# One hybrid transformer block on one core: the interleaving tables of all five engines written anew

## The reference

```
x = x + deltanet(layernorm(x))      # 8 heads of 16, two decaying states per head, scan over the tokens, own output norm
x = x + layernorm(x) @ sign(W).T
x = x + attention(layernorm(x))     # 16 heads of 8, rotary q and k, causal softmax, projection
x = x + layernorm(x) @ sign(W).T
```

## Time and profile before

| | |
|---|---|
| median of three executions | 686.31 us |
| all three | 686.31, 685.63, 686.48 us |
| span of the profiled execution, first to last instruction | 679.2 us |
| what the median has beyond that span | 7.1 us |
| TensorE busy (matmul) | 587.1 us, 86% |
| VectorE | 542.6 us, 80% |
| ScalarE | 414.9 us, 61% |
| GpSimd | 216.5 us, 32% |
| share of the last-ending chain: TensorE, VectorE, issue, DMA | 34%, 27%, 14%, 9% |
| mean granted TensorE clock | 0.955 |

### The profile page before, as it was taken

One profiled execution on the slowest core, in us unless ns is written; L12 is line 12 of the kernel. 1 busy time (PEld: TensorE's weight loads), 2 busy tenths in 40 slices (PEclk: granted clock), 3 DMA queues, 4 the chain that ended last, 5 costly groups with the idle time before them and its releaser, 6 DMA issues.

```text
span 679.2 us, 16869 instructions
## 1 busy us (share of the span) xinstructions
PE 587.1 (86%) x6352; PEld 338.2 (50%) x6352; DVE 542.6 (80%) x1547; ACT 414.9 (61%) x884; POOL 216.5 (32%) x255
## 2 busy tenths in 40 slices
PE   3686876888989899999999999999999999788995
PEld 2344534445545555555644655464646554434543
DVE  5677774889877988889899879898799877966842
ACT  2754652545777467864795767775695566346583
POOL 5261631353243251434432521535033531000000
PEclk9689787599989999999999999999999999979999
DMA  3710027000460035201540054005400433054000
GB/s 118 120 22 1 17 74 111 7 18 2 92 112 6 10 82 90 47 3 34 104 88 1 27 111 77 15 10 112 76 15 27 83 57 46 18 103 74 18 19 15
DMA packets 24914, 35.07 MB, mean 52 GB/s; under 512 B 4857, under 2 KB 22265, under 8 KB 22521
## 3 DMA queue, kind: packets, MB, share of 16 engines
q1 hardware_dynamic: 24834, 34.01, 25.4%
HBM read 22.85 MB, written 8.39 MB: 46 GB/s over the span
## 4 chain that ended last, share of the span: by engine, by line
PE 34%; DVE 27%; issue 14%; DMA 9%; POOL 7%; ACT 6%; SPq 2%; POOLq 0%; DVEq 0%; ACTq 0%
DVE mrow L1679 8%; DMA qs<-consts_bf 7%; PE ps L1215 5%; PE ps L1167 4%; PE ps L912 4%; DVE qkf L1629 3%; PE ps L1199 2%; PE ps L1196 2%; PE ps L1169 2%; PE ps L992 2%; SPq L543 2%; DVE am L1504 2%; POOL xe L624 2%; PE ps L907 2%; DMA scratch<-parts 1%
## 5 line engine op out<-in xcount | busy, mean ns | idle before, releaser
L1679 DVE TENSOR_REDUCE mrow<-ps 128x1 f32<-128x384 f32 (+3 forms) x352 | 220.5, 634 | 66.6 <-PE ps L1169 64.2
L873 ACT ACTIVATE pT<-ps 128x512 f32<-128x512 f32 (+1 forms) x330 | 173.9, 556 | 94.9 <-PE ps L1199 84.4
L1167 PE MATMUL ps<-ks,qs 72*128 72x128 bf16 (+2 forms) x384 | 101.2, 284 | 25.1 <-DVE mrow L1679 23.3
L1169 PE MATMUL ps<-ks,qs 123*128 123x128 bf16 x512 | 92.2, 226 | 6.2 <-DMA qs<-consts_bf 4.6
L1199 PE MATMUL ps<-qs,ks 75*128 75x256 bf16 (+2 forms) x384 | 93.8, 276 | 0.0
L1196 PE MATMUL ps<-qs,ks 123*128 123x128 bf16 x512 | 88.7, 223 | 5.2 <-ACT pT L873 2.4
L1215 PE MATMUL ps<-pT,va 128*32 128x512 f32 (+1 forms) x960 | 89.4, 449 | 1.8 <-DVE xk L1736 0.7
L636 POOL TENSOR_TENSOR spread<-state,cst 128x144 f32<-128x144 f32 x112 | 47.3, 444 | 121.1 <-DVE state L1533 85.1
L1167 PEld LDWEIGHTS ps<-ks,qs 72*128 72x128 bf16 x384 | 36.8, 98 | 96.7 <-DVE mrow L1679 85.8
L1196 PEld LDWEIGHTS ps<-qs,ks 123*128 123x128 bf16 x512 | 45.4, 98 | 60.9 <-ACT pT L873 26.3
L593 POOL TENSOR_TENSOR mid_rstd<-mid_ve,half 128x4 f32<-128x4 f32 x24 | 28.7, 1194 | 138.5 <-DVE mid_ve L1317 138.5
(11 more groups left out here) (209 smaller groups left out, 1091.5 us busy)
## 6 DMA issues: line engine op xcount, KB each, us to landing
ks<-scratch SPq DMA_DIRECT2D x48, 192.0 KB
scratch<-parts SPq DMA_DIRECT2D x48, 128.0 KB, 1.8
qs<-scratch SPq DMA_DIRECT2D x32, 128.0 KB
qs<-scratch SPq DMA_DIRECT2D x16, 192.0 KB
x<-x SPq DMA_DIRECT2D x8, 256.0 KB, 3.3
qs<-scratch SPq DMA_DIRECT2D x32, 64.0 KB
out<-xk SPq DMA_DIRECT2D x8, 256.0 KB, 2.3
qs<-pT SPq DMA_DIRECT2D x3, 384.0 KB, 9.2
```

Source lines behind the costliest of these rows:

```text
L873: act.activation(probs(b, g, kt)[:, c0:c0 + m, :], ps[:, score_bank(b, n), 0:m * width].rearrange("p (m n) -> p m n", n=width), ACT.Exp, s ...
L1167: pe.matmul(o[:, 0:qt * P], qs[0:K_MAX, f % RING, h, own_tile], ks[0:K_MAX, f % RING, h, 0:qt * P], start=True, stop=True, skip_group_chec ...
L1169: mm = pe.matmul(o[:, own_tile], qs[0:K_DIAG, f % RING, h, own_tile], ks[0:K_DIAG, f % RING, h, own_tile], start=True, stop=True, skip_gro ...
L1679: dve.tensor_reduce(mrow[:, qt, h0:h0 + m], ps[:, max_banks(b)[n % len(max_banks(b))], 0:m * width].rearrange("p (m k) -> p m k", k=width) ...
```

## The change

All five strings are written anew. They hold the same letters, each as often, so every step is done once, on the same engine, with the same instructions and waits; only its place among the other streams' steps is another. Nothing else differs, except that `SP_ORDER` now fills three lines of the file, so each later line has a number two higher (L1169 before is L1171 now). On each engine the coarse order stays: which batch is in which stream beside which other. On TensorE 763 of 1285 steps stand in short stretches in which the order differs, on VectorE 705 of 1073, on ScalarE 309 of 708, on GpSimd 101 of 176 and on SyncE 20 of 96. Most are swaps over one to five steps; the norm steps (n) of batches 4 to 7 move furthest.

One row of ScalarE's string, the one in which the n of batch 7 stands (the last n of the string, before and now), and the string of SyncE:

```
 ACT_ORDER = (
...
-    "ssmasassasssssaaasaaaamaaasamxssamseanssaessamamsamaassaaaaaasaaxamasaaaaaaasasaassaamasasaassaasasasasa"
+    "asssaasssssssaasaaaaaaamasamaxsssemassseaasammamsaaaassaaaaasaanxamsaaaaaaasaasaassaaamassasasaasasasasa"
...
-SP_ORDER = "nxnmmmmmmmmnxmmmmmmmxnmxmmammmmmxnmxammmmmmmxnmxmmmmmammxnmxmammmmmmxmxmmmmmammxmmxmmmmmmxmxaxaa"
+SP_ORDER = (
+    "nnxmmmmmmmmnxmmmmmmmxnmxmammmmmmxnmxmmmammmmxnmxmmmmmammxnmxmmmmmammxmxmmmmmmmaxmxmmmmmmmxmxxaaa"
+)
```

More of the change, by code:

```diff
@@ new lines @@
+    "sxsaexsaexsaaxsxxssxsxaaaxasaaxsxaxasxasxaxaaaxmasxmxaasxaaxaaaaxsxasaxamxaaaxaasaxasxaasxaxassxmxaaaxas"
+    "xaaxasaxsasxaasxasaaxssxaaxaamxaaxsexmsssxsxsexmxsxsxesxasxsasaxexsxssxsxesxesaxasxaaxaxaasaxasxmxssxaaa"
+    "saaxamsamaaxaasasaaamxasxaaaxaaamsxasxaxsaaxasaxaaxasxaxasxsxaaxmsaxmaxasaaaxasxmxaaxasasxaasxssexssxsmx"
+    "esxsxeasxeaxsssxessaxesxsxasxssxaaxaaxasaxsaxsaaxsxaaxaamxaasaxaxamaaxsaaaxasxaaaaxasxamaxaaxaxasaamxaas"
+    "xsxaxxassxaaxsxsaaxsaxaaaxsaaxaaxamsxaaxsemsxxsxemxssssexasxasexmaexsxsxaaexssxsaxasxsxasaxsaxsxasxsaxsx"
@@ new lines @@
+    "snmsmmmmmmsmsssssssssssssssssssssxsxxssxsxsxmxsxsmxmmxmxsxsxmxssxsmxsxmxssxsmmxssxssmxxxxxsnmsnxsxsssxns"
+    "snmxsxmmmxsxssxssxssmxmxmsxssxmmxmxssmxssxxxmssxmxmsssmxxsxxxmmsmmxxsxmmxnxsxxsxmsxmxsmmmxsmxxxsxssxssns"
+    "xsaxamxmasxmxaxxxxsxmmxnsxasxsssxsaxanaaxmxssxaxxsssxsxsxsxmxssxsxsxxmxmxssmxxsxmxxmmmxmxssxsxssxmnxsxsm"
+    "xmxmxxmxsxsnxmssxxmsmxsxxnsxxaxaxxnmxsxsmsxsxssxaaxmxsxsmxssxssxssxasxaxaaaxmxamxsxsxsssssxxxsssmxsxxssx"
+    "xxmmmmmsmmmssxsmxssxnxmsmxsxmxmxmnmxnxmsxxsxnsxsxmxmxmxsxmxmxssxxxxxssssaxassxaaxsxmsxaxasssxsassxsaaxxs"
@@ L133 @@
+    "axxsxssxsxmssxxssxssxxxxxxxxmmsmmssmxmxmxmxmxssxsxssmxnxsxsmxxxxmxmxsxmmsmxsxsxsnxxxnxaxaxmmxmxassxamsxm"
+    "xsassxssxaxanmaaxsxaxssxsxssxssxxsxsxxsxsssxssmxxxxsxsssxmxmxmmsxmsxsxmxmxxssxsxsxsxmxmsxsmmxxmxmxmmmxsx"
+    "sxxxxxssaxasmmxssamxamxmxmxsxasxsaxssxasxsxaasxxaxsxsxsssxsxmxssxssxssxxxssxxssssxxmxmmxmxmmxmxmxmmmxxmx"
+    "mxmmxmxxxxxmxmxmxxaxaxmxmaxaxmxmxaxaxmxaaaxmxaxmxmxxxxxxxxxxxxxxxxxxxxxxxxxxxxxxxxxxxxxxxxxxxaaxxaxaxxxx"
+    "xxxxxxxxxxxxxxxxxaaaaaaaaaaaaaaaa"
 )
 POOL_ORDER = (
-    "nnssssnssnsssssmnmsssmsssssssnnsxssmnssssmssnsmnsxsmmmmmnsnssmsmssssmasmsmnmsxmnmssmnsssssmssnammmssxmnm"
```

46 lines of the change are left out of this document (16 added, 30 removed).

## The result

The changed kernel takes 716.58 us (median of four runs, 715.06 to 723.77), the kernel before 685.97 beside it: a ratio of 1.0496, 95% interval 1.0433 to 1.0558. It is slower by some 31 us, and 27 us above the upper end of the predicted range.

A forecast was written before the change was run, and what follows sets the result against it. Only idle time could be won, at most TensorE's 92.1 us of 679.2. Terms 0.75 - 0.8 - 0.5 + 0 - 1.0 + 0 - 0.8 = -2.35 us took the median 686.31 to 684.0 us, range 679.0 to 690.0.

The forecast's parts named there:

- GpSimd costed at nothing: Scan 0: GpSimd's norm step of batch 1 moves behind two spread steps, claimed to cost nothing.
- Scan 0, masks on ScalarE: Scan 0: the mask copy now stands between the last `qM` and `qp`, delaying `am`; +0.75 us, bounds 0 and 1.00.
- Rotary tables: Scan 0, VectorE: table work of 0.92 us moves behind the next state update; -0.8 us, bounds 0 and -0.92.
- xn on ScalarE: Scan 0: xn of batch 1 (1.64 us) now follows `yT`; -0.5 us, bounds 0 and -1.64.
- First maxima: Near 108 to 118 us: q projection and `ytok` turn go ahead, but waits return later; 0, bounds -1.35 and +0.9.
- The steady part: The remaining swaps around maxima groups, reductions and attention scores, 107 to 550 us; -1.0 us, range -6 to +5.
- the fill that comes back: Slower rival: steps put before maxima groups delay reductions, five places +4.5 us; 690.3 us, chance 0.28.
- Late norms: Norm steps of batches 4 to 7 wait longer in the queues, covered by a ScalarE hole; 0 us.
- the tail: Batch 6's `xk` sum, copy and feed-forward leave the front of batch 7's last maxima and turn; -0.8 us, bounds -1.0 and 0.
- The clock: Rival: the fill keeps TensorE at full clock from 119.4 to 136.5 us, 3.1 us more gain; 681.0 us, chance 0.11.

The follow-up runs named there:

- GpSimd cut short: Both kernels with every long GpSimd tensor instruction cut to four elements, output left out: changed order 692.56 us, order before 684.10 us.
- GpSimd reading nothing: Both kernels with GpSimd's long tensor instructions replaced by memsets of the same length, values left out: changed order 690.69 us, order before 678.63 us.
- the old end in place: The changed kernel with GpSimd's tensor instructions cut to four elements and the orders of before from about 560 us on: 688.27 us.

## Why the prediction was wrong

**The bound.** "No instruction is added or taken away, so what an order can win is idle time alone" is the sentence that failed. It took durations as given. The order also sets which instructions of VectorE and GpSimd run at the same time, and with it how long VectorE's take: 25 us of lengthening came on top of 7. Every term was costed with durations of the old neighbourhood, and the range, made of moved idle time, could not hold the result. The trace of before showed the effect, and I read past it. The subtraction at L1374 ran beside a decay block and took 1.92 us where its twin L1373 took 0.28:

```profile
33.89 0.28 DVE L1373 TENSOR_SCALAR w<-w,wmean 128x128 f32<-128x128 f32 x1
33.95 1.97 POOL L624 TENSOR_TENSOR xe<-lpart,hot 96x1024 bf16<-96x1024 bf16 x1
34.08 1.92 DVE L1374 TENSOR_SCALAR vec<-vec,wmean 128x128 f32<-128x128 f32 x1
```

**GpSimd costed at nothing.** "TensorE did not wait for `xe` there, so I cost this at nothing; the cover is the work in TensorE's own queue." GpSimd's own order is the same up to there (spread, decay block, `xnb`, spread, spread), and it was VectorE's copies that moved, from behind the decay block at 33.95 us to a place beside it. Then the norm step of batch 1, which stood at 41.39 us between a spread and the next decay block, has gone behind both. So that block now starts 0.77 us after the spread (44.07 and 44.84) and not 2.24 (40.62 and 42.86), and runs beside VectorE's tables, where before VectorE had nothing to do from 41.75 to 45.02 us. The cost that I put at nothing for TensorE went to VectorE, in instructions that do not wait for GpSimd's results.

**Scan 0, masks on ScalarE: +0.75 expected, +2.97 measured.** `am` started at 34.71 and not at 31.74. The product that `am` reads starts 2.25 us later (32.69 against 30.44). The second exponent product, for which I had seen the wait for the masks and costed nothing, starts at 30.04 and not at 29.46, and most of the rest is the set-up product on TensorE, which I took for a help: it is behind the exponent products, but still ahead of the product that `am` reads. That product itself takes 1.98 us and not 1.17, since from 21.3 to 35.0 us the granted clock is now at 0.50; before, that stretch ended at 30.7. In the changed kernel, and last the same product before:

```profile
30.04 0.59 PE L979 MATMUL ps<-xe,own 128*128 128x512 bf16 x1 [0.52 <-ACT pT L848]
30.84 1.49 PE L1083 MATMUL ps<-w,mean_w 128*128 128x384 f32 x2 [0.22 <-issue]
32.12 0.64 PE L1084 MATMUL ps<-sgn,mean_w 128*128 128x128 f32 x2
32.69 1.98 PE L994 MATMUL ps<-qM,kT 128*64 128x512 f32 x4
...
30.44 1.17 PE L992 MATMUL ps<-qM,kT 128*64 128x512 f32 x4
```

I had counted only what it moved away from. With GpSimd cut short this delay was down to 0.5 us by 110 us, so in itself it is worth little.

**Rotary tables: -0.8 expected.** The tables did leave the place in front of the state update. At the new one, their first eight instructions take 3.21 us and not 0.92, for GpSimd's next decay block runs there from 44.84 us and two spreads behind it:

```profile
44.78 3.21 DVE L1398 TENSOR_SCALAR x<-cst 128x64 f32<-128x64 f32 x8
47.89 0.41 DVE L1516 TENSOR_TENSOR kd<-ktok,dec 128x256 f32<-128x256 f32 x1
```

**xn on ScalarE: -0.5 expected, about -0.7 measured.** The changed kernel is 6.56 us behind at that `kd` (47.89 against 41.33) and 5.90 at the `yT` behind which xn now stands (55.51 against 49.61). Other moved steps lie between the two, so the 0.7 is not shown to be xn's alone.

**First maxima: right in what was worked out.** The waits ahead of the second, third and fourth group are 0.79, 0.83 and 0.79 us, where I had said about 0.7, and the wait for the DMA is gone. The group itself starts 3.18 us behind the projection's start (120.71 to 123.89), and not the 5.98 of my sum, because the clock was full there and the two projections took 2.05 and 1.02 us in place of 2.90 and 2.02.

**The steady part: -1.0 expected, bounds -6 to +5.** From 107 us on the new orders lost 19 to 23 us. The rival with the right sign, the fill that comes back, was priced at 690.3 (its terms, 4.5 less 1.35 at start and tail, give 689.5). It is not the main cause: with GpSimd reading nothing the same orders, with the same fills, take 26 us less. But it is not ruled out as a part. Its sign of recognition, more waiting of TensorE for the maxima, did appear (15.2 to 27.1 us from 107 to 550 us), and some of it is there without the port: 19.0 us against 15.1 of the old order with GpSimd cut short, 22.0 against 15.0 with the memsets. In these two pairs the new order loses some 2 and 5 us from 107 to 550 us. So the steady term without the port came out with the other sign, inside its bounds or at their upper end; the port is what took it far out of them.

**Late norms and tail.** GpSimd's `xk` of batch 7 waited 64.70 us for the store and ended at 691.29; less the 34 us by which everything is late there, that is 657.3, where I had said 657.5, and the context of batch 7 at 701.03 did not wait for it. These dependences were read rightly. The 0.8 us of the tail came and went again. At the turn of `mparts` the changed kernel is 33.35 us behind (684.29 against 650.94), 0.6 less than where the reductions before it begin (673.65 against 639.69). But the first scores of the second half are 34.06 behind (689.37 against 655.31). The feed-forward of batch 6, which I had as out of the way, now stands right in front of them, and they no longer wait for the DMA:

```profile
688.42 1.11 PE L914 MATMUL ps<-sgn,xkT 128*128 128x128 f32 x8
689.37 0.22 PE L1198 MATMUL ps<-qs,ks 123*128 123x128 bf16 x1
```

**The clock: left out of the sum.** It was a rival on the better side only, at 3.1 us for a stretch. By some 4 to 6 us it went the other way: in the profiled executions the half-clock stretches sum to 98.0 us and not to 61.4. The runs make it second to the port: with GpSimd reading nothing the ten executions have a granted clock of 0.950 in the mean against 0.932, which by the 2.6 us for 0.01 is some 5 of the 26 us that are gone.

Some 4 to 8 us are not settled (688.3 against 684.1 by the medians, 1.0015 against 0.9892 by the ratios): what stays between the two orders with GpSimd out of the way and the old end in place. Their mean clocks are alike (0.963 in twelve executions, 0.961 in four), and the two profiled executions are only 1.2 us apart (spans of 682.9 and 681.7), at 0.980 and 0.962. The fills that come back are a candidate; no run separates them.

## What to carry to other kernels

Before an order is changed, mark in the trace which VectorE instructions run beside a GpSimd one, and group them by where their operands are; an instruction that reads PSUM is a safe neighbour, one with two SBUF inputs or a copy on SBUF is not. Compare the longest with the shortest of each form: where they differ, durations are not constants, and a sum of old durations cannot price a new order. An order that was tuned on the chip may owe part of its time to quiet neighbourhoods (the kernel before has 7.0 us of lengthening, every changed one with its results intact has more), and a shift of one engine against the other can lose them.

## What the runs showed of the hardware

- A GpSimd sum on SBUF holds up VectorE instructions with two SBUF inputs, copies and one-input arithmetic on SBUF for the rest of its length (three sums of 128x4 in a row: 0.29 us alone, 1.04 beside it); a GpSimd memset holds up only the last two kinds; forms with an input in PSUM are held up by neither (0.28, 0.68 and 0.28 us beside every kind).
- GpSimd gives some back: beside 128x512 sums of VectorE its second and third sum took 1.71 us in place of 1.26.
- 88 sums of 1.03 us each on an engine that was idle two thirds of the time made this kernel 5.4% slower; 88 memsets of 0.95 us, 2.4%.
- Among executions of one kernel, those with a higher granted clock are shorter: 682.65 us at 0.96 or more, 688.99 at 0.945 or less.
- A piece of a quarter of the elements took 0.62 us where the whole took 1.89, and several pieces in a row held one VectorE instruction up for 2.3 us.
